# A Mamba-style scan overlapped with an expert layer: each chunk's gram made in the slot of the y products ahead of it

## What is computed

```python
proj = rmsnorm(hidden) @ w_in_proj          # z, x, B, C, dt_raw
x = silu(conv4(x));  dt_h = softplus(dt_raw @ w_dt + b_dt) averaged per head
# scan over chunks, 8 heads, state 64, head width 32
lcs  = cumsum(dt_c * A)
M    = exp(where(lower_triangle, lcs[l] - lcs[i], -inf))
G    = einsum('blhn,bihn->bhli', C_c, B_c)                   # the gram
y    = einsum('bhli,bihp->blhp', M * G, x_c) + exp(lcs) * C_c @ h
h    = exp(lcs[-1]) * h + einsum(M[-1], x_c, B_c)
out1 = x0 + residual + rmsnorm((y + x * D) * silu(z)) @ w_out_proj
# expert layer on layernorm(out1): 2 shared and 4 routed blocks, top 2 of 4
hidden_b = relu(f @ w1 + b1);  out = out1 + sum_b weight_b * (hidden_b @ w2 + b2)
```

## Time and profile before

| | |
|---|---|
| time, median of 3 runs | 580.51 us (578.98 to 584.52) |
| the profiled execution's own time | 576.64 us |
| its span in the trace | 574.9 us |
| PE busy | 548.7 us, 95% of the span |
| DVE, ACT, POOL busy | 437.6, 356.2 and 172.6 us |
| DMA queue q1, share of 16 engines | 25.9% |

### The profile page before, as it was taken

One profiled execution on the slowest core, in us unless ns is written; L12 is line 12 of the kernel. 1 busy time (PEld: TensorE's weight loads), 2 busy tenths in 40 slices (PEclk: granted clock), 3 DMA queues, 4 the chain that ended last, 5 costly groups with the idle time before them and its releaser, 6 DMA issues.

```text
span 574.9 us, 11864 instructions
## 1 busy us (share of the span) xinstructions
PE 548.7 (95%) x4016; PEld 429.8 (75%) x4016; DVE 437.6 (76%) x1037; ACT 356.2 (62%) x767; POOL 172.6 (30%) x232
## 2 busy tenths in 40 slices
PE   8886999999999999999999999999999999999996
PEld 7665767877777777877787777777778787777774
DVE  4878767887789785888688786987768787676654
ACT  3894488637675477636795477745787376852442
POOL 2073504521163202631046201622036210542011
PEclk9999999999999999999999999999999999999999
DMA  6650006300550006600272004700064003510120
GB/s 204 183 152 2 0 33 190 84 1 2 147 173 3 1 6 175 143 1 0 81 173 65 0 0 155 164 0 0 15 198 106 0 1 105 157 44 1 38 59 21
DMA packets 37354, 41.43 MB, mean 72 GB/s; under 512 B 3482, under 2 KB 27716, under 8 KB 37316
## 3 DMA queue, kind: packets, MB, share of 16 engines
q1 hardware_dynamic: 36724, 40.80, 25.9%
q10 hardware_dynamic: 592, 0.15, 0.1%
HBM read 37.79 MB, written 3.15 MB: 71 GB/s over the span
## 4 chain that ended last, share of the span: by engine, by line
PE 48%; DVE 19%; issue 11%; ACT 9%; DMA 5%; POOL 5%; SPq 1%; DVEq 0%; ACTq 0%; POOLq 0%
PE bank L424 7%; PE bank L426 5%; PE bank L425 5%; PE bank L535 4%; PE bank L642 4%; PE bank L644 4%; PE bank L643 4%; DVE act_l L1268 4%; DVE cv L1121 4%; DMA grow<-lc_rows 3%; ACT act_h L874 3%; PE bank L547 2%; PE bank L563 2%; PE bank L435 2%; ACT L967 2%
## 5 line engine op out<-in xcount | busy, mean ns | idle before, releaser
L1268 DVE SCALAR_TENSOR_TENSOR act_l<-bank,act_h 128x512 fp32r<-128x512 f32 x192 | 131.3, 686 | 69.8 <-ACT act_h L874 68.6
L874 ACT ACTIVATE act_h<-bank 128x512 fp32r<-128x512 f32 x192 | 114.1, 594 | 81.9 <-PE bank L426 78.0
L424 PE MATMUL bank<-fTl,w1h 128*128 128x512 f32 x192 | 86.9, 452 | 3.0 <-DVE fTl L1219 2.3
L1492 POOL TENSOR_TENSOR late<-late 128x512 f32<-128x512 f32 x31 | 39.8, 1285 | 163.3 <-DVE late L1276 163.3
L894 ACT ACTIVATE seg<-seg,lneg 128x128 f32<-128x128 f32 x256 | 81.2, 391 | 2.8 <-DMA seg<-lc_rows 2.8
L642 PE MATMUL bank<-act_l,w2h 128*128 128x512 f32 x192 | 77.5, 404 | 1.6 <-DVE act_l L1268 1.5
L425 PE MATMUL bank<-fTh,w1l 128*128 128x512 f32 x192 | 75.7, 394 | 0.0
L644 PE MATMUL bank<-act_h,w2h 128*128 128x512 f32 x192 | 75.6, 394 | 0.0
L426 PE MATMUL bank<-fTh,w1h 128*128 128x512 f32 x192 | 75.6, 394 | 0.0
L643 PE MATMUL bank<-act_h,w2l 128*128 128x512 f32 x192 | 75.2, 392 | 0.0
L1479 POOL TENSOR_TENSOR xw<-xs,seg 128x128 f32<-128x128 f32 x48 | 19.9, 414 | 157.3 <-ACT seg L894 82.8
(11 more groups left out here) (176 smaller groups left out, 1063.6 us busy)
## 6 DMA issues: line engine op xcount, KB each, us to landing
seg<-lc_rows SPq DMA_DIRECT2D x32, 512.0 KB, 4.5
late<-gk_rows SPq DMA_DIRECT2D x8, 1024.0 KB, 9.3
grow<-lc_rows SPq DMA_DIRECT2D x48, 128.0 KB, 5.4
x_in<-L_attn_hidden_dram SPq DMA_DIRECT2D x8, 256.0 KB, 3.7
out_dram<-late SPq DMA_DIRECT2D x8, 256.0 KB, 2.5
late<-L_ffn_sw_dram SPq DMA_DIRECT2D x2, 512.0 KB, 7.2
late<-L_ffn_rw_dram SPq DMA_DIRECT2D x1, 1024.0 KB, 7.7
CT<-L_attn_w_in_proj_dram SPq DMA_DIRECT2D x1, 512.0 KB, 5.3
```

Source lines behind the costliest of these rows:

```text
L424: mm(dst, stat_h, mov_l, start=True, stop=False)
L874: nc.scalar.activation(act_h[:, b % RING, :], HID[b % 2][:], ACT.Relu).then_inc(act_h_ready, 1)
L1268: v_.scalar_tensor_tensor(act_l[:, r, :], HID[b % 2][:], 0.0, f(act_h[:, r, :]), ALU.max, ALU.subtract)\
```

## The change

1. `dta` and `kept` get 32 columns for each chunk in place of 8 and 4 (the rest zeros, set once). So `lcs` makes its transposed sums with one full matmul, and `g_transposes` with one transpose.
2. `gram(s, c + 1)` is issued inside `y_product(s, c)`, behind the state product, for c = 0 to 2. Only gram(0) keeps its place at step 1. The y product itself waits for mg only in the last chunk, since elsewhere the gram ahead of it has waited.
3. On DVE the two mg halves of chunks 1 to 3 stand behind the act_l of step 0 and behind the act_l of step 1. Chunk 0, and all chunks of sequence 0, keep both at step 1.
4. On ACT the last `b_copy` comes ahead of slot 6's relu, and the first `xs_copy` moves from slot 5 to slot 6.
5. On DVE slot 2 has one convolution tap and slot 3 three, in place of two and two.

```diff
-        dta = sb("dta", [P, (NCH - 1) * NH + 32])
+        dta = sb("dta", [P, NCH, 32])
...
-                mm(sums[:, 0:32], upto[:], dta[:, 0:32], start=True, stop=True)
-                for c in range(NCH):
-                    ins = mm(sums[32 * c:32 * c + 32, P:2 * P], dta[:, c * NH:c * NH + 32], upto[:], start=True, stop=True)
-                ins.then_inc(lcs_psum, 1)
+                mm(sums[:, 0:32], upto[:], dta[:, :, 0:NH], start=True, stop=True)
+                mm(sums[:, P:2 * P], dta[:].rearrange("p c q -> p (c q)"), upto[:], start=True, stop=True).then_inc(lcs_psum, 1)
...
                     ins.then_inc(s_psum, 1)
+                if c < NCH - 1:
+                    gram(s, c + 1, None)
                 if c > 0:
                     pe.wait_ge(y_steps, nth(s, 8, 2 * c))
...
-                    if b == 0:
+                    if b == 0 and c == NCH - 1:
                         pe.wait_ge(mg_ready, nth(s, 8, 2 * c + 2))
...
-                for c in range(NCH):
-                    ins = mm(MAIN[2][32 * c:32 * c + 32, 0:P], kept[:, c * NE:c * NE + 32], ident[:], start=True, stop=True)
-                ins.then_inc(gT_psum, 1)
+                nc.tensor.transpose(MAIN[2][:, 0:P], kept[:].rearrange("p c q -> p (c q)"), ident[:]).then_inc(gT_psum, 1)
...
-                    if step == 1:
+                    if step == 1 and c == 0:
                         gram(s, c, prev)
...
+                    if s is not None and i == 6:
+                        b_copy(s, 3)
                     if new := block_at(i, prev, older):
                         relu(*new)
-                    if s is not None and i in (5, 6):
-                        b_copy(s, i - 3)
-                        xs_copy(s, i - 5)
+                    if s is not None and i == 5:
+                        b_copy(s, 2)
+                    if s is not None and i == 6:
+                        xs_copy(s, 0)
+                        xs_copy(s, 1)
...
+            def masked_gram(s, c, hf):
+                dve.wait_ge(g_psum, nth(s, 8, 2 * c + hf + 1))
+                dve.wait_ge(decay_masked, nth(s, 8, 2 * c + hf + 1))
+                if hf == 0 and (v := nth(s, 4, c)) is not None:
+                    dve.wait_ge(y_psum, v)
+                v_.tensor_tensor(mg[:, hf], MAIN[2 + hf][:].rearrange("p (n l) -> p n l", n=NP), decay(c)[:, hf], ALU.mult)\
+                    .then_inc(mg_ready, 1)
...
-                if step == 1:
...
+                if step == 1 and (c == 0 or is_seq(s, 0)):
+                    masked_gram(s, c, 0)
+                    masked_gram(s, c, 1)
...
                     if (new := block_at(i, prev, older)) and not (i == 0 and prev is not None):
                         act_low(*new)
+                    if s is not None and i in (15, 18, 21):
+                        masked_gram(s, i // 3 - 4, 0)
+                    if s is not None and i in (16, 19, 22):
+                        masked_gram(s, i // 3 - 4, 1)
...
-                            conv(s, 1, (0, 1))
+                            conv(s, 1, (0,))
                         if i == 3:
-                            conv(s, 1, (2, 3))
+                            conv(s, 1, (1, 2, 3))
```

More of the change, by code:

```diff
@@ L180, in build @@
         rank = sb("rank", [P, NCH * NE])
-        kept = sb("kept", [P, (NCH - 1) * NE + 32])
+        kept = sb("kept", [P, NCH, 32])
         gT = sb("gT", [P, P])
@@ L704, in scan_part @@
                         b_tokens(s, c, prev, older)
-                    if step == 1:
+                    if step == 1 and c == 0:
                         gram(s, c, prev)
-                        if c == NCH - 1 and not is_seq(s, n_seq - 1):
-                            proj(s + 1, 0)
+                    if step == 1 and c == NCH - 1 and not is_seq(s, n_seq - 1):
+                        proj(s + 1, 0)
                     if step == 2:
@@ L785, in opening @@
                         b_tokens(0, c, None, None)
-                    gram(0, c, None)
+                    if c == 0:
+                        gram(0, c, None)
                     if c < 2:
@@ L1138, in dt_decay @@
                 dve.wait_ge(dt_steps, nth(s, 3, 2))
-                v_.tensor_tensor(dta[:, 0:NCH * NH].rearrange("p (c h) -> p c h", h=NH), dsum[:].rearrange("p (c h) -> p c h", h=NH),
+                v_.tensor_tensor(dta[:, :, 0:NH], dsum[:].rearrange("p (c h) -> p c h", h=NH),
                                  a_neg[:].unsqueeze(1).to_broadcast([P, NCH, NH]), ALU.mult).then_inc(dt_steps, 1)
@@ L1144, in c_copy @@
                 v_.tensor_copy(CT[:, b, :], MAIN[b][:]).then_inc(c_ready, 1)
-            def attend(s, c, step):
-                if step == 1:
[L1148 to L1154, removed]
+            def masked_gram(s, c, hf):
[5 more added lines that the diff above has]
+                    .then_inc(mg_ready, 1)
+            def attend(s, c, step):
+                if step == 1 and (c == 0 or is_seq(s, 0)):
+                    masked_gram(s, c, 0)
+                    masked_gram(s, c, 1)
                 if step == 2:
@@ L1254, in top_two @@
                 step(8)
-                v_.scalar_tensor_tensor(kept[:, 0:NCH * NE], rank[:], 1.5, gw_n[:].rearrange("p c e -> p (c e)"),
+                v_.scalar_tensor_tensor(kept[:, :, 0:NE], rank[:].rearrange("p (c e) -> p c e", e=NE), 1.5, gw_n[:],
                                         ALU.is_lt, ALU.mult).then_inc(gate_kept, 1)
@@ L1431, in opening @@
                                 channel_multiplier=1).then_inc(tables_set, 1)
-                for t, v in ((ones[:], 1.0), (upto[:], 1.0), (turn[:], 0.0), (lower[:], 1.0), (center[:], -1.0 / P), (dta[:, NCH * NH:], 0.0), (kept[:, NCH * NE:], 0.0)):
+                for t, v in ((ones[:], 1.0), (upto[:], 1.0), (turn[:], 0.0), (lower[:], 1.0), (center[:], -1.0 / P), (dta[:, :, NH:], 0.0), (kept[:, :, NE:], 0.0)):
                     g.memset(t, v).then_inc(zeros_set, 1)
```

## The result

The changed kernel takes 618.34 us (median; 616.72 to 619.1) where the kernel before takes 580.73: a ratio of 1.066 (95% interval 1.062 to 1.071). The direction was forecast; the size was not: + 38 us instead of + 17.

The account below looks back on a forecast made before the run. PE's own stream, busy 95%, was taken as the bound. Waits of 4.32 us less gains of 0.45, 0.50 and 0.67 gave + 2.70 a period, + 16.9 in total: 597 us, range 586 to 605.

Parts of the forecast that it names:

- the walk: Step-by-step timing of PE, ACT and DVE through chunks 1 to 3 of one period; net + 2.70 us a period.
- The new wait: Moved gram (slots 17, 20) and slot 23's y product wait for mg's second half: 1.42, 1.76, 1.14 us, 4.32 a period.
- The last sequence's chunk 3: No projection or norm1 for a successor follows there, so its wait was put 0.6 us shorter.
- Not all of this survives: Ahead of the scan, act_l at slot 9 limits what PE gains; 0.67 us a period kept for the whole part.
- the two smaller groups: The lcs matmuls and kept transposition ahead of the scan get shorter: together 0.5 us a period if nothing takes it back.
- The gram moves: Chunks 1 to 3: moving the gram beside the y product saves tiling form changes, 0.15 us three times, 0.45 a period.
- The count of changes: Alternative count by the tiling drain rule: three form changes a chunk instead of four, gain 0.10, total forecast 1 us higher.
- the end of the period: PE's act_l wait there goes, as act_l is then in time: 0.5 us a period given back.
- Sum: Adds + 4.32, - 0.45, - 0.50, - 0.67 to + 2.70 us a period, + 18.9 for seven, + 16.9 in total.
- (a): Rival: chunk 3's segment and growth rows also arrive late, up to 1 us a period more, 604 us; chance 0.18.
- (b): Rival: ACT is not late, only floor waits remain, 2.24 us a period, 583 us; chance 0.12.
- (c): Rival: the wait for mg does not bind and the kernel gets faster, 568 us; chance 0.07.

Follow-up runs that it names:

- run with early rows and filled waits: Changed kernel, growth rows raised behind the relu (slots 12, 15), rows issued before the old store, dummy matmuls in slots 17, 20, 23: 600.78 us, ratio 1.039.
- filled run that keeps slot 14's wait: Changed kernel with four dummy matmuls ahead of each moved gram of sequences 1 to 7: 608.35 us, ratio 1.052.
- the small edits alone: Kernel before with only the wider dta and kept tiles, the b_copy and xs_copy order and the convolution taps: 579.19 us, ratio 1.002.
- the chain is cut: Kernel before with wider tiles, copy order, taps, growth rows behind the relu and rows issued before the old store: 571.86 us, ratio 0.986.
- the split alone: Kernel before with only the mg halves of chunks 1 to 3 placed behind act_l of steps 0 and 1, gram unmoved: 595.22 us, ratio 1.031.
- the fill: Dummy full-array matmuls put where PE waits: changed kernel 608.35 us; with growth rows behind the relu and rows before the store too, 600.78 us.
- kernel with the smaller waits: Changed kernel with growth rows raised behind the relu (slots 12, 15) and rows issued before the old store, no dummy matmuls: 615.4 us, ratio 1.067.

## Why the forecast was right in direction and wrong in size

**The bridge.** The seven periods grew by 38.6 us, 18.3 were forecast. The run with early rows and filled waits has neither slot 14's wait nor a drop, and stands 19.7 above the kernel before: as a whole program it takes 600.8 us, where 597 was forecast. The filled run that keeps slot 14's wait has 7.6 more (495.3 - 487.7), and the clock has nearly all of the other 11.3 (506.6 - 495.3). So 19.7 + 7.6 + 11.3 = 38.6. What the walk left out, 18.9, was as much as the whole forecast. That the rest meets the forecast to 1.4 us is in part luck. An undisturbed period of that run is 3.2 us longer than one of the kernel before (69.4 against 66.2), where 2.70 was forecast, and three of the kernel before's own periods are longer than 66.2, by 0.4 to 4.3, the longest with a drop of the clock. The opening adds 3.85 to the miss: + 2.85 where - 1.0 was forecast, with idle times of 1.95 and 1.13 us for mg and a drop from 39.3 to 46.1 there. The kept transposition at the end, 0.4 forecast and nothing found, adds the rest.

**"The new wait": right.** Chunk 1 was forecast at 1.42 and measured 1.42, chunk 3 1.14 and 1.13. Chunk 2 was 1.50 instead of 1.76: relu 19 came 0.12 earlier behind its slot's transposes, and PE reached the gram 0.14 later. The half-made mg, the idle DVE, the relu behind the decays all stand in the trace as walked. *The first of the two steps that failed is what this part left out:* it walked chunks 1 to 3 and not chunk 0, where gram(1) waits for mg(0), and so put slot 14 at nothing. Both halves of mg(0) keep their order, and I took that for no change. But its slack was 0.05 us, and PE was about to come 0.5 us earlier. Slot 14 has 9.6 us of idle time in six of the seven periods. The last sequence's chunk 3, put at 0.6 us less, waits no less than the others (1.07 us idle against 0.95).

**"Not all of this survives": the wrong limit.** The gain ahead of the scan was 0.49 us against 0.67 forecast, the two smaller groups had it without the BT order and the tap, and it did not survive at all: I looked for what is late next in slot 9 and stopped there. The next late thing was six slots on. That the small edits alone give 1.002 shows it, and that they give 0.54 a period once the chain is cut shows it from the other side.

**"The gram moves": right in kind, and small.** From L519 to L545 chunk 1 takes 3.22 us; before it was 4.51 with the gram, 3.42 without its 1.09. So 0.20 us is saved in chunk 1, and 0.18 in chunk 2. In chunk 3 nothing is: there the next sequence's first matmul (L424, of hTl) now starts 0.39 us behind the one ahead of it and not 0.23, and the one behind it 0.33 later, and the stretch from L442 to L557 is 1.01 shorter, less than the gram's 1.09. That makes 0.30 a period where 0.45 was taken. In its new place the gram begins 0.93 behind L545 (302.77 - 301.84), just as L557 does behind L547 in the kernel before. The Trainium skill ("TensorEngine Tiling (Array Packing)", Key Properties) says that a change of tiling mode drains TensorE. The steps of 0.10 agree, and the 0.93 does not speak against it: the last record of L545 starts at 302.56, 0.21 ahead of the gram, where those records are 0.11 apart. The count of changes gave 0.10 a chunk; the three chunks measured 0.20, 0.18 and -0.08, which is 0.10 on average, but not for the reason counted.

**"The new wait", the end of the period:** 0.50 was taken for the act_l wait that goes, 0.23 came. That y_psum comes later cost nothing that the trace shows.

**"Sum": the clock.** *This is the second step that failed, and the larger.* Every price was taken at the full clock because the earlier trace rows show 1.00, in a period in which PE idles 1 us of 66. The change adds waits of 0.8 to 2.6 us, three or four to a period, and in six of the seven periods the granted clock then fell to 0.50. The term stands at nothing in the sum, and measured 10 to 12 us; no walk of one period shows it.

**The rivals.** (a) took its 0.22 us for the transfer's wait from one quiet period; the kernel before has 1.1 to 1.7 in four of seven. Its mechanism shows in the split alone, with 0.1 to 0.5 us, but in the changed kernel ACT's need moved with PE as the text said. A chain of the same kind decided slot 14, in a chunk that (a) did not look at. (b) and (c) fell with the first waits. What stays open: why the transfer of the rows took 0.6 us longer, and which wait brings a drop. Idle times of 1.41 and 1.42 us had one behind them, and those of 1.31 to 1.42 in the undisturbed period had none.

## What to carry to other kernels

Before pricing a gain ahead of a loop, walk from it to the first consumer with almost no slack, however many slots away, and chunk 0 with the rest; a transfer read by an in-order engine ahead of a relu is part of that walk. When two instructions swap on an engine, ask what the one now ahead waits for: here act_l's wait for a relu cost some 30 us. And when a change puts several idle microseconds on a nearly full PE, price the lower clock as a case of its own, and put dummy matmuls in the gap to measure it.

## What the runs showed of the hardware

The granted clock of a PE that is 90% busy fell to 0.50 for 3.4 us at a time, six times in seven periods, around waits of 1.4 to 2.6 us; with the fill in the waits the periods were 11.3 us shorter in one pair of traces and 12.0 in the other, and in both no drop was left in them. In the second pair that is 1.5 us for each stretch of 3.4. The kernel with the smaller waits (25.9 us for mg at the gram, against 33.2) had eight drops against six. The Trainium skill ("TensorE: Matmul & The Clock Gate", A second HAM failure mode: psum-queue depth-cycling) tells of a kernel whose frequent short idle times make the clock go up and down; the trace agrees, and here the short idle times are semaphore waits.

Work added to the full engine can make a kernel faster: 84 more matmul records over the whole run, and 8 to 10 us less.
